# First attention: queries and keys in fp32, 32 columns per head, and scores as fp32 matmuls over 16 rows in place of bf16 stacks

## The reference

```python
q = (x @ Wq.T).reshape(N, L, H, D).transpose(0, 2, 1, 3)
k = (x @ Wk.T).reshape(N, L, H, D).transpose(0, 2, 1, 3)
v = (x @ Wv.T).reshape(N, L, H, D).transpose(0, 2, 1, 3)
q = _layernorm(q, gq, bq)
k = _layernorm(k, gk, bk)
scores = jnp.einsum('nhld,nhmd->nhlm', q, k) * SM_SCALE
if CAUSAL:
    causal = jnp.tril(jnp.ones((L, L), dtype=bool))
    scores = jnp.where(causal, scores, NEG)
attn = jax.nn.softmax(scores, axis=-1)
out = jnp.einsum('nhlm,nhmd->nhld', attn, v)
out = out.transpose(0, 2, 1, 3).reshape(N, L, EMB)
return out @ Wo.T + bo
```

## Time and profile before

| | us |
|---|---|
| median of three runs | 4109.65 |
| lowest and highest | 4104.24, 4113.88 |
| span of the profiled execution | 4099.4 |

### The profile page before, as it was taken

One profiled execution on the slowest core, in us unless ns is written; L12 is line 12 of the kernel. 1 busy time (PEld: TensorE's weight loads), 2 busy tenths in 40 slices (PEclk: granted clock), 3 DMA queues, 4 the chain that ended last, 5 costly groups with the idle time before them and its releaser, 6 DMA issues.

```text
span 4099.4 us, 93010 instructions
## 1 busy us (share of the span) xinstructions
PE 3512.7 (86%) x31392; PEld 2772.0 (68%) x31392; DVE 3056.1 (75%) x6444; ACT 2303.1 (56%) x6346; POOL 776.0 (19%) x919
## 2 busy tenths in 40 slices
PE   3898988989889898898988889888898988989888
PEld 2676766767667676676766767666676766767667
DVE  3878777787777877768787787877778777787776
ACT  2656546565465664646655465654656546565464
POOL 1212222022120221212122121222202212022120
PEclk9999999999899999999999999998999989999899
DMA  3000000000000000000000000000000000000000
GB/s 73 7 2 7 7 7 7 2 7 7 7 7 1 8 6 7 7 7 7 2 7 7 7 7 2 7 7 7 7 2 7 7 7 7 2 7 7 6 1 6
DMA packets 33906, 30.35 MB, mean 7 GB/s; under 512 B 8864, under 2 KB 33312, under 8 KB 33376
## 3 DMA queue, kind: packets, MB, share of 16 engines
q1 hardware_dynamic: 33376, 23.68, 2.0%
HBM read 15.28 MB, written 8.39 MB: 6 GB/s over the span
## 4 chain that ended last, share of the span: by engine, by line
PE 56%; issue 14%; DVE 13%; ACT 10%; POOL 5%; SPq 1%; ACTq 0%; DMA 0%; DVEq 0%; POOLq 0%
PE bank L619 12%; PE scores L717 9%; ACT prob L833 6%; PE bank L630 6%; PE scores L606 6%; PE bank L729 5%; PE scores L607 4%; PE scores L608 3%; POOL qf L499 2%; PE scores L691 2%; PE scores L671 2%; PE scores L602 2%; PE bank L590 2%; DVE negmax L1049 1%; DVE stk L1145 1%
## 5 line engine op out<-in xcount | busy, mean ns | idle before, releaser
L833 ACT ACTIVATE prob<-scores,negmax 128x128 f32<-128x128 f32 (+3 forms) x2048 | 1060.8, 538 | 223.6 <-DVE negmax L1049 180.2
L1049 DVE TENSOR_REDUCE negmax<-scores 128x1 f32<-128x128 f32 (+3 forms) x2048 | 884.5, 483 | 102.0 <-PE scores L608 88.4
L619 PE MATMUL bank<-ident,prob 128*128 128x128 f32 x5120 | 731.2, 280 | 44.5 <-DVE probt L1057 35.1
L1057 DVE COPY probt<-bank 128x512 f32<-128x512 f32 x896 | 596.6, 683 | 180.1 <-PE bank L619 173.1
L619 PEld LDWEIGHTS bank<-ident,prob 128*128 128x128 f32 x5120 | 548.6, 142 | 155.5 <-DVE probt L1057 65.9
L606 PE MATMUL scores<-khh,qt 128*128 128x256 f32 (+2 forms) x1024 | 439.2, 430 | 13.3 <-issue 6.6
L608 PE MATMUL scores<-mask,ident 128*128 128x128 bf16 x2048 | 450.4, 231 | 0.0
L833 ACT ACTIVATION_READ_ACCUMULATOR prob<-scores,negmax 128x1 f32 x2048 | 438.0, 214 | 0.0
L804 ACT ACTIVATE probt<-bank 128x512 f32<-128x512 f32 x384 | 233.0, 607 | 205.3 <-PE bank L619 205.3
L607 PE MATMUL scores<-kll,qt 128*128 128x256 f32 (+2 forms) x1024 | 346.1, 338 | 0.0
L590 PE MATMUL bank<-ident,stk 128*96 128x128 bf16 x2048 | 206.9, 288 | 149.8 <-DVE stk L1147 119.7
(11 more groups left out here) (178 smaller groups left out, 6937.0 us busy)
## 6 DMA issues: line engine op xcount, KB each, us to landing
x_in<-in_x_rows SPq DMA_DIRECT2D x16, 512.0 KB, 3.5
out_rows<-x SPq DMA_DIRECT2D x16, 512.0 KB, 3.5
r_gu<-in_wg SPq DMA_DIRECT2D x2, 512.0 KB, 5.1
r_gu<-in_wu SPq DMA_DIRECT2D x2, 512.0 KB, 5.1
r_d<-in_wd SPq DMA_DIRECT2D x1, 1024.0 KB, 6.5
r_wqt<-in_wq_nope_t SPq DMA_DIRECT2D x1, 512.0 KB, 6.8
r_wqr<-in_wq SPq DMA_DIRECT2D x2, 256.0 KB, 8.6
r_wob<-in_wo SPq DMA_DIRECT2D x1, 512.0 KB, 5.3
```

The source lines that it names most:

```text
L619: ins = nc.tensor.transpose(bank[4 + n % 2][:, q * P:(q + 1) * P], prob[:, u % 2, q, i * P:(i + 1) * P], ident[:, :])
L833: nc.scalar.activation(prob[:, u % 2, q, 0:n], bank[q][:, 0:n], ACT.Exp, bias=negmax[:, a, u, q:q + 1], accum_out=sums[:, a, u, q:q + 1]). ...
L1049: nc.vector.tensor_reduce(negmax[:, a, u, M * part:M * part + M], scores[:, M * part:M * part + M, 0:n], axis=AX.X, op=ALU.max, negate=Tru ...
L1057: nc.vector.tensor_copy(probt[:, u % 2, i], bank[4 + n % 2][:, :]).then_inc(probt_dve.sem, 1)
```

## The change

The tiles qkt, stk and res1 go, and with them the ACT and DVE work that fills them. The offset is now written straight to a tile `wide`, in fp32, with 32 columns per head of which 16 are used. PE transposes four heads at once (128 columns), 8 transposes per token tile. ACT copies the queries and DVE the keys into `qk1`, so that head q of a group has its 16 rows in the 32-row strip q. A score is one fp32 product over these 16 rows; the mask product stays. POOL sets `wide` to zero once, and waits for the transposes of tile t - 2 before it writes the offset of tile t.

```diff
-    qkt = new("qkt", [SD, 2 * H, L], BF16)
+    qk1 = new("qk1", [P, 2, NG, L], F32)
+    place[0] += 16384
     qt = at("qt", [P, H, L], F32R, region_q)
+    wide = at("wide", [P, 2, 2, H, HP], F32, region_q + 16384)
...
-    res1 = at("res1", [P, 2, 2 * C], F32, o + 8192)
-    stk = at("stk", [P, 2, 2 * H, SPLITS, D], BF16, o + 12288)
...
+        nc.gpsimd.memset(wide[:, :, :, :, :], 0.0)
         nc.gpsimd.memset(va[:, :, :, :], 0.0).then_inc(va_zeroed, 1)
...
-                nc.gpsimd.tensor_tensor(v, v, bet[:, :, :].unsqueeze(2).to_broadcast([P, 2, H, D]), ALU.add).then_inc(qhat_ready.sem, 1)
+                if t >= 2:
+                    pool.wait_ge(wide_psum.sem, wide_psum.at(b, 2 * (t - 1)))
+                nc.gpsimd.tensor_tensor(wide[:, s, :, :, 0:D], v, bet[:, :, :].unsqueeze(2).to_broadcast([P, 2, H, D]), ALU.add).then_inc(qhat_ready.sem, 1)
...
-        def transpose_stack(b, t):
-            pe.wait_ge(stack_ready.sem, stack_ready.at(b, t + 1))
-            for quad in range(4):
-                n = 4 * t + quad
-                if n >= 4:
-                    copied = stackt_dve if quad % 2 else stackt_act
-                    pe.wait_ge(copied.sem, copied.at(b, (n - 4) // 2 + 1))
+        def transpose_wide(b, t):
+            pe.wait_ge(qhat_ready.sem, qhat_ready.at(b, t + 1))
+            for w in range(2):
+                n = 2 * t + w
+                if t >= 2:
+                    copied = wide_dve if w else wide_act
+                    pe.wait_ge(copied.sem, copied.at(b, t - 1))
                 else:
-                    pe.wait_ge(v_ready.sem, v_ready.at(b, quad + 1))
-                out = bank[4 + quad].bitcast(BF16)
-                for i in range(8):
-                    ins = nc.tensor.transpose(out[0:SD, i * P:(i + 1) * P],
-                                              stk[:, t % 2, quad * 8 + i].rearrange("p s d -> p (s d)"), ident16[:, :])
-                ins.then_inc(stackt_psum.sem, 1)
+                    pe.wait_ge(v_ready.sem, v_ready.at(b, n + 1))
+                for g in range(NG):
+                    ins = nc.tensor.transpose(bank[4 + n % 4][:, g * P:(g + 1) * P],
+                                              wide[:, t % 2, w, g * G:(g + 1) * G].rearrange("p h d -> p (h d)"), ident[:, :])
+                ins.then_inc(wide_psum.sem, 1)
...
                 if a == 0:
-                    mm(bank[q][:, 0:n], qkt[:, h, j * P:(j + 1) * P], qkt[:, H + h, 0:n], start=True, stop=False)
+                    rows = slice(q * HP, q * HP + D)
+                    mm(bank[q][:, 0:n], qk1[rows, 0, g, j * P:(j + 1) * P], qk1[rows, 1, g, 0:n], start=True, stop=False)
...
-        def copy_stack(b, t):
-            for quad in (0, 2):
-                act.wait_ge(stackt_psum.sem, stackt_psum.at(b, 4 * t + quad + 1))
-                copy(qkt[:, quad * 8:(quad + 1) * 8, t * P:(t + 1) * P],
-                     bank[4 + quad].bitcast(BF16)[0:SD].rearrange("p (h t) -> p h t", h=8)).then_inc(stackt_act.sem, 1)
+        def copy_wide(b, t):
+            act.wait_ge(wide_psum.sem, wide_psum.at(b, 2 * t + 1))
+            copy(qk1[:, 0, :, t * P:(t + 1) * P], bank[4 + 2 * t % 4].rearrange("p (g t) -> p g t", g=NG)).then_inc(wide_act.sem, 1)
...
-                t = step - 2
-                if 0 <= t < NT:
-
-                    s = t % 2
-                    act.wait_ge(qhat_ready.sem, qhat_ready.at(b, t + 1))
-                    if t >= 2:
-                        act.wait_ge(stackt_psum.sem, stackt_psum.at(b, 4 * (t - 1)))
...
-                    copy(stk[:, s, 0:H, 0:3], qv.to_broadcast([P, H, 3, D]))
-                    copy(stk[:, s, H:2 * H, 0:4:3], kv.to_broadcast([P, H, 2, D]))
-                    copy(stk[:, s, H:2 * H, 5], kv[:, :, 0]).then_inc(part1_ready.sem, 1)
                 if step >= 3:
-                    copy_stack(b, step - 3)
+                    copy_wide(b, step - 3)
```

More of the change, by code:

```diff
@@ L41 @@
 NM = G // M
-SPLITS = 6
-SD = SPLITS * D
 R = 32
@@ L266, in _build @@
     qhat_ready = Signal(sem("qhat_ready"), NT)
[L267 to L271, removed]
+    wide_psum = Signal(sem("wide_psum"), 2 * NT)
+    wide_act = Signal(sem("wide_act"), NT)
+    wide_dve = Signal(sem("wide_dve"), NT)
     kv_psum = Signal(sem("kv_psum"), 1)
@@ L323, in _build @@
     act_link = sem("act_link")
-    DVE_LINKS, POOL_LINKS, ACT_LINKS = 28, 18, 4
+    DVE_LINKS, POOL_LINKS, ACT_LINKS = 20, 18, 4
     block = ctx.enter_context(nc.Block())
@@ L742, in sequence @@
             for t in range(NT):
-                transpose_stack(b, t)
-            pe.wait_ge(stackt_act.sem, stackt_act.at(b, 2 * NT))
-            pe.wait_ge(stackt_dve.sem, stackt_dve.at(b, 2 * NT))
+                transpose_wide(b, t)
+            pe.wait_ge(wide_act.sem, wide_act.at(b, NT))
+            pe.wait_ge(wide_dve.sem, wide_dve.at(b, NT))
             attend(b, 0)
@@ L1032, in split_tokens, with copy_wide @@
                 tt(xtl[:, k], bank[TOKEN_BANK[stage] + k][:, :], xth[:, k].bitcast(F32), ALU.subtract).then_inc(xtl_ready.sem, 1)
-        def copy_stack(b, t):
-            for quad in (1, 3):
-                dve.wait_ge(stackt_psum.sem, stackt_psum.at(b, 4 * t + quad + 1))
-                nc.vector.tensor_copy(qkt[:, quad * 8:(quad + 1) * 8, t * P:(t + 1) * P],
-                                      bank[4 + quad].bitcast(BF16)[0:SD].rearrange("p (h t) -> p h t", h=8)).then_inc(stackt_dve.sem, 1)
+        def copy_wide(b, t):
+            dve.wait_ge(wide_psum.sem, wide_psum.at(b, 2 * t + 2))
+            nc.vector.tensor_copy(qk1[:, 1, :, t * P:(t + 1) * P],
+                                  bank[4 + (2 * t + 1) % 4].rearrange("p (g t) -> p g t", g=NG)).then_inc(wide_dve.sem, 1)
         def copy_q(b, n):
@@ L1135, in sequence @@
                     chain.link(tt(v, v, gam[:, :, :].unsqueeze(2).to_broadcast([P, 2, H, D]), ALU.mult))
-                    tt(v, v, bet[:, :, :].unsqueeze(2).to_broadcast([P, 2, H, D]), ALU.add).then_inc(qhat_ready.sem, 1)
-                t = step - 2
-                if 0 <= t < NT:
-                    s = t % 2
-                    dve.wait_ge(part1_ready.sem, part1_ready.at(b, t + 1))
-                    rv = res1[:, s].rearrange("p (h d) -> p h d", d=D)
-                    chain.link(tt(rv, qn[:, s].rearrange("p (h d) -> p h d", d=D), stk[:, s, :, 0], ALU.subtract))
-                    nc.vector.tensor_copy(stk[:, s, 0:H, 3:5], rv[:, 0:H].unsqueeze(2).to_broadcast([P, H, 2, D]))
-                    chain.link(nc.vector.tensor_copy(stk[:, s, H:2 * H, 1:5:3], rv[:, H:2 * H].unsqueeze(2).to_broadcast([P, H, 2, D])))
-                    tt(stk[:, s, 0:H, 5], rv[:, 0:H], stk[:, s, 0:H, 3], ALU.subtract)
-                    tt(stk[:, s, H:2 * H, 2], rv[:, H:2 * H], stk[:, s, H:2 * H, 1], ALU.subtract).then_inc(stack_ready.sem, 1)
+                    tt(wide[:, s, :, :, 0:D], v, bet[:, :, :].unsqueeze(2).to_broadcast([P, 2, H, D]), ALU.add).then_inc(qhat_ready.sem, 1)
                 if step >= 3:
-                    copy_stack(b, step - 3)
+                    copy_wide(b, step - 3)
             attend(b, 0)
```

2 lines of the change are left out of this document (removed).

## The result

The changed kernel takes 5283.89 us (median, 5267.6 to 5292.49) against 4111.36 (4104.24 to 4113.88) for the kernel before on the same chip: a ratio of 1.286 [1.282, 1.291], 28.6% slower. The profiled execution spans 5278.3 us, 1178.9 more than the earlier trace rows. The forecast was 4565 in a range of 4320 to 4700: right in sign, and only two fifths of the loss.

The account below looks back on a forecast made before the run. PE was taken to bound the changed first attention: +36.9 us a pass there and -8.5 in the preparation, over 16 passes 454 us on the profiled 4099.4, plus 10 for the median, gave 4565 us, range 4320 to 4700.

Parts of the forecast that it names:

- What bounds it: First attention after the change: PE sets a 22.5 us period per group; ACT and DVE fit with ease.
- The price of a score: First attention: 2.18 us of stream plus 0.37 us a tile for one head, 14.6 us for a group.
- Two changes of shape: Between strip score and full-row mask, PE needs 0.09 us each way, 0.18 us a head.
- Weights: First fp32 weights of a score have nothing to lie beside after a change of shape: 0.107 us exposed.
- The fp32 stream: Each fp32 score runs as two passes: 0.218 us for 128 columns, 0.87 for 512.
- Preparation: Stage before the first score: casts, copies and transposes go, POOL's chain remains; -8.5 us a pass (-7 to -10).
- I add 3 us (0 to 5): First attention's start: the lower clock level, today hidden by waits, costs a bound PE 3 us a pass.
- Four new periods: First attention's four groups at the new period: 90.0 us, giving 88.9 for the stage before the clock allowance.
- Low bound: First attention: no PE stop between strip and full rows gives 4340 us; first weights hidden too, 4215.
- The clock: Rival: 16-row streams lower the attention's clock; 5850 us at 1.2 GHz throughout, 5010 for half; chance 0.12.
- side by side: Rival: a unit's four strip scores overlap in the first attention, which stays at 55.0 us; total 3974; chance 0.04.
- No stop between shapes: Rival: PE does not stop between strip and full rows in the first attention; 4215 to 4440 us, chance 0.17.

Follow-up runs that it names:

- 5: Changed kernel with each score over 32 rows, the further 16 cleared to zero each pass, one strip at a time: 5278.61 us, against 4113.13 before.
- experiment 2: Changed kernel with the score product over 64 rows, summing two heads' strips, same sequence: 4845.2 us.
- 3: Changed kernel with the score product over all 128 rows, summing four heads, so no change of shape: 4344.47 us, against 4108.44 before.
- Experiment 1: Changed kernel with a unit's four strip scores issued one behind the other, their four masks after them: 4330.05 us, 1.054 times the kernel before.
- 6: Changed kernel with four strips issued together, masks after, each strip over 32 rows with zeros in the further 16: 4287.02 us, 1.0435 times the kernel before.
- 7: Against 6, the last unit's products with the values stand ahead of the next unit's scores in the first attention: 4586.4 us, 1.116 times the kernel before.
- experiment 4: Changed kernel with one to four added 128-row, 512-column bf16 products ahead of each score, overwritten by it: 5371.3 us.
- experiment 8: Changed kernel's preparation in bf16, with one bf16 score product over all 128 rows, summing four heads: 3996.24 us, 0.972 times the kernel before.
- experiment 9: Changed kernel's preparation in bf16, with one-pass bf16 scores over the head's 16-row strip: 4179.01 us, against 4109.4 before.

## Why the prediction was wrong

The granted clocks of the first attention side by side, worked out from the records of passes 2 to 15 of each kernel:

| kernel | rows in use by the scores | first attention, us | clock | lower level ahead of the first rise, us | and after it, us |
|---|---|---|---|---|---|
| before | 96, bf16 | 54.5 | 0.99 | 0.8 | 0 |
| changed | 16, one strip | 134.8 | 0.63 | 36.6 | 64.1 |
| 5 | 32, one strip | 135.0 | 0.63 | 37.3 | 64.1 |
| 2 | 64 | 108.2 | 0.81 | 32.3 | 8.3 |
| 3 | 128 | 76.5 | 0.97 | 4.8 | 0 |
| 1 | 16 in each of four strips | 76.0 | 0.79 | 20.1 | 12.2 |
| 6 | 32 in each of four strips | 72.8 | 0.91 | 13.1 | 0 |
| 7 | as 6, with longer waits of PE | 91.2 | 0.81 | 11.0 | 23.6 |
| 4 | 16, with full-row products between | 141.5 | 0.87 | 37.0 | 0 |
| 8 | 128, bf16 | 55.4 | 0.95 | 5.7 | 0 |
| 9 | 16, one strip, bf16 | 65.8 | 0.88 | 16.0 | 0 |

*What bounds it.* Right: PE, busy throughout, ACT and DVE near 40%, no other engine next.

*The price of a score.* Right, at the higher level of the clock. Heads of the changed kernel start 0.58, 0.79 and 1.00 us apart at 128, 256 and 384 keys (1194.92 to 1195.50, 1199.56 to 1200.35, 843.18 to 844.18). At 512 keys the changed kernel is never at the higher level, but with the added products of experiment 4 a head takes 2.08 - 4 x 0.213 = 1.23 us, and in experiment 2, with the same sequence, 125 of the 192 distances are 1.22 us at that level. The sum is 3.60 us, against the forecast's 2.18 + 4 x 0.37 = 3.66. Its parts are close too. Two changes of shape: 0.18 forecast, 0.20 in experiment 9. Weights: a 512-key head costs 0.97 without changes and 1.23 with them, so 0.26 for changes and exposed weights, forecast 0.18 + 0.107; with 0.20 for the changes, some 0.06 is left for the weights. The fp32 stream is two passes at 0.85 ns a column each (0.218 us for 128 columns), as L630's rows said.

What the forecast did not ask is how a price moves with the clock. At 256 keys a head takes 0.79 us at the higher level and 1.37 at the lower, which is 0.58 more and not 0.79 more. The 0.21 that stays is the two changes of shape. In experiment 9 a 512-key head takes 0.48 and 0.75 us: 0.27 doubles, and 0.21 stays again. So a change of shape costs about 0.1 us at either level, and the lower level less than doubles such a head.

*Preparation.* Right: 25.6 us, 7.7 less, forecast 8.5 less. POOL's offsets are 4.76 us apart, forecast 5.15, and the last stands third from the end of the preparation, before the transposes and one copy:

```profile
1082.26 1.26 POOL L452 TENSOR_TENSOR wide<-qn,bet 128x512 f32<-128x512 f32 x1 [0.16 <-POOL qn L449]
...
1087.02 1.26 POOL L452 TENSOR_TENSOR wide<-qn,bet 128x512 f32<-128x512 f32 x1 [0.16 <-POOL qn L449]
...
1090.33 0.69 DVE L977 COPY qk<-bank 128x512 f32<-128x512 f32 x1 [3.63 <-PE bank L548]
1091.17 0.76 PE L561 MATMUL scores<-qk 16*128 16x128 f32 x2 [0.88 <-DVE qk L977]
```

*The failed step* is one of the sum: "I add 3 us (0 to 5)", the whole allowance for the clock. It took the clock at 0.97 from the earlier trace rows of a stage whose scores use 96 rows, into a stage whose scores use 16, and priced only the start of the stage. The stage should have been 91.9 us; it was 134.8, and 16 x 42.9 = 686 us is nearly the whole miss of 719 (the rest is the preparation's 0.8 us a pass, 13 us, and small change in the other stages). Where the forecast put the price of the lower level at 0 to 5 us a pass, it is 43 on top of the 3. The start that it did see lasts 36.6 us at the lower level and not the few of today, and another 64.1 us come after it, which it did not see at all.

Two smaller slips had no part in this. The forecast read the second attention as 59.4 us, but that window of the earlier trace rows ends at 1027.0, and the attention's output projection starts at 1030.36; the mean is 63.6, so its edges add 3.1 us to four periods of 15.12 and do not take 1.1 off. Four new periods are then 93.1 us with nothing for the clock, close to the 91.9 used. And the sums of the Low bound come to 4352 and 4242 by their own terms, where 4340 and 4215 are written.

*The rival "The clock"* (0.12) is what happened. A mean clock of 0.63 is three quarters of the time at 0.50 and the rest at 1.00, and 5284 lies between the two cases worked out there, half of the time (5010) and throughout (5850). The "4900 and more" that it had for its chance held. The argument against it was a wrong inference from a right row. The six 8-column products of the earlier trace rows did stand ahead of a clock of 0.99; they are narrow, but use all 128 rows. I read "small shapes count" out of it and carried it to products with few rows. Experiments 2 and 3 change nothing but the rows (and, in 3, the changes of shape) and the clock goes from 0.63 to 0.81 to 0.97. Experiment 4 keeps the 16 rows and all changes and adds full-row work, and it goes to 0.87. Few rows alone are not the whole condition either: in bf16 (experiment 9) 16 rows delay the rise, and the clock then stays up. That the chip counts rows is not shown by this; what is shown is that the rows, in this sequence of fp32 products, decide between the two levels.

*The rival "side by side"* (0.04) was rightly set aside for this change, and for the right reason, the mask between. Experiment 1 moves the masks and the strips overlap. But its price was wrong by more than 300 us: "attention would stay at 55.0" forgot that the strips of a unit then wait for their banks and that the clock is lower (0.79), with 20.1 us of the lower level at the stage's start and 12.2 later. At 76.0 us it would have been slower than before as well, 4330 and not 3974.

*"No stop between shapes"* (0.17) is out, by experiment 9.

What is not settled: why one strip gives the same clock with 16 and 32 rows, while four strips together do not (0.79 and 0.91); and why the full-row products of experiment 4 keep the clock up but do not make it rise any earlier (37.0 us against 36.6). The products that four strips have at work together span 64 rows (16 in each) and 128 (32 in each), which stands close to the clocks of experiments 2 and 3 (0.81, 0.97), but the two pairs also differ in PE's waits, and no run took these apart. A 128-row fp32 score that is a head's own was not tried either: it needs copies of one operand with zeros in the other strips, and experiment 8 shows only what the preparation would bring beside it.

## What to carry to other kernels

Price a product with few rows twice: at both levels of the granted clock. When PE is to become the bound and most of its time goes to products on 16 or 32 rows, a row of a stretch with full-row products does not tell the level; look for a stretch with as few rows at work, and where there is none, give the lower level a large chance. Ask at which level the stage before hands over: a stage that begins at the lower level and runs such products stays there long (36.6 us here, 4.8 with 128 rows), even where it keeps the higher level once it has it. Small row strips pay only when they are issued back to back with their banks free; a full-row product between them, such as this mask, ends the overlap and adds about 0.1 us each way, at either level.

## What the runs showed of the hardware

- The granted clock of a PE that hardly waited (under 0.4 us in the stage) went with the rows that its score products used: 0.63, 0.63, 0.81 and 0.97 for 16, 32, 64 and 128 rows in the same sequence. Adding 34 us of full-row products a pass cost 6.7 us, for the clock rose from 0.63 to 0.87.
- Coming from a preparation that left it at the lower level, the clock rose after 4.8 us with scores on 128 rows, 16.0 with bf16 scores on 16 rows, and 36.6 with fp32 scores on 16 rows.
- A change between a 16-row strip and full rows and back costs 0.20 us at the higher level (experiment 9) and 0.21 at the lower, with whatever weights it leaves exposed. The Trainium skill, "TensorEngine Tiling (Array Packing)", Key Properties, says that a change of tiling mode drains TensorE and gives no time; the trace agrees that such a change costs time, and gives it.
- Four fp32 strips of 256 columns overlapped in 0.64 us, 2.7 times as fast as the 1.72 us of four streams one after the other. A strip whose bank ACT had not yet read waited for it (1.95 us for the next unit, of 384 columns).
